# Layer 1 attention: key projections taken from among the scores into the weighing

## The reference, cut to what matters

```python
q = split(xn @ Wq)                                # 16 heads, 1024 x 64
k = concat([split(xn @ Wkv[:, :1024]), split(ctx @ Wm)])
v = concat([split(xn @ Wkv[:, 1024:]), split(ctx @ Wm)])
attn = softmax(q @ k.T * 64 ** -0.5)              # 1024 x 7428 for each head
x = x + tanh(g) * (heads(attn @ v) @ Wo + bo)
```

## Time and profile before

| | |
|---|---|
| median of 3 runs | 5230.36 us (5229.31 to 5230.93) |
| profiled execution, its own time | 5229.35 us |
| its span | 5227.6 us |
| PE busy in the span | 4813.3 us (92%) |
| DVE busy | 4069.5 us (78%) |
| ACT busy | 3357.1 us (64%) |
| POOL busy | 1961.0 us (38%) |
| L960, projections, in the stretch 440 to 2700 us | 238 matmuls |
| L1018, weighing | 3024 matmuls |

### The profile page before, as it was taken

The page is one execution under the profiler, slowest core; times in us unless marked ns, Lnnn a source line. Parts: engine busy times, 40 slices in busy tenths (PEclk is TensorE's granted clock), DMA queues, the critical chain, the costliest instruction groups (busy, mean ns, idle before and its releaser), DMA issues. The chain is left out here.

```text
span 5227.6 us, 76770 instructions
## 1 busy us (share of the span) xinstructions
PE 4813.3 (92%) x26366; PEld 1882.8 (36%) x26366; DVE 4069.5 (78%) x4870; ACT 3357.1 (64%) x6623; POOL 1961.0 (38%) x1522
## 2 busy tenths in 40 slices
PE   8938999999999999999994699999998699999997
PEld 5623454545445454544442222222222222222222
DVE  7646767677676767677776699999995599999996
ACT  3314565666666566656651388888885288888886
POOL 0015878787787878788782100000000100000000
PEclk9978999999999999999996799999998699999998
DMA  1024334242333334242210311111110211111110
GB/s 36 5 88 120 95 95 112 63 123 54 110 75 99 95 90 117 55 126 56 52 30 16 81 32 29 29 29 29 29 23 2 79 29 29 29 32 32 29 23 6
DMA packets 171390, 298.23 MB, mean 57 GB/s; under 512 B 39060, under 2 KB 108576, under 8 KB 167392
## 3 DMA queue, kind: packets, MB, share of 16 engines
q1 hardware_dynamic: 169420, 292.95, 22.0%
q10 hardware_dynamic: 1584, 0.37, 0.0%
HBM read 187.39 MB, written 101.25 MB: 55 GB/s over the span
## 5 line engine op out<-in xcount | busy, mean ns | idle before, releaser
L1856 ACT ACTIVATE a_prob<-ps 128x512 f32<-128x512 f32 (+1 forms) x3264 | 1699.4, 602 | 289.0 <-PE ps L1736 284.2
L1914 DVE TENSOR_REDUCE a_mx<-ps 128x1 f32<-128x1024 f32 x1536 | 1815.1, 1220 | 70.6 <-PE ps L1748 55.0
L1283 POOL TENSOR_TENSOR tot_p<-tot_p,prob 128x512 f32<-128x512 f32 (+1 forms) x922 | 1300.6, 1411 | 353.6 <-ACT prob L1141 267.6
L1748 PE MATMUL ps<-a_K,a_Q 59*128 59x512 bf16 (+1 forms) x3328 | 1094.7, 386 | 56.6 <-DMA a_Q<-q_stack_dram 44.7
L1141 ACT ACTIVATE prob<-ps 128x512 f32<-128x512 f32 (+1 forms) x1512 | 801.4, 609 | 511.7 <-PE ps L1007 510.7
L1736 PE MATMUL ps<-a_Q,a_K 59*128 59x512 bf16 (+1 forms) x3264 | 988.7, 383 | 55.3 <-ACT a_prob L1856 49.1
L1772 PE MATMUL ps<-a_prob,a_V 128*9 128x512 f32 x6528 | 872.1, 596 | 10.9 <-ACT a_acc L1840 10.9
L1006 PE MATMUL ps<-QA,KA 128*128 128x512 f32 (+1 forms) x1888 | 841.7, 446 | 0.0
L1018 PE MATMUL ps<-prob,V 128*64 128x512 f32 x3024 | 801.1, 599 | 0.7 <-ACT prob L1141 0.7
L1007 PE MATMUL ps<-QB,KB 128*128 128x512 f32 (+1 forms) x1888 | 746.6, 395 | 0.0
L1224 DVE TENSOR_TENSOR tot_d<-tot_d,prob 128x512 f32<-128x512 f32 x539 | 619.4, 1149 | 146.0 <-ACT prob L1141 129.5
(11 more groups left out here) (419 smaller groups left out, 4341.4 us busy)
## 6 DMA issues: line engine op xcount, KB each, us to landing
a_K<-k_stack_dram SPq DMA_DIRECT2D x128, 300.2 KB
k_hi_dram<-hi_s SPq DMA_DIRECT2D x112, 256.0 KB, 2.1
k_lo_dram<-lo_s SPq DMA_DIRECT2D x112, 256.0 KB, 2.4
KA<-k_hi_dram SPq DMA_DIRECT2D x64, 384.0 KB, 4.3
KA<-k_lo_dram SPq DMA_DIRECT2D x64, 384.0 KB, 5.6
KB<-k_hi_dram SPq DMA_DIRECT2D x64, 384.0 KB, 6.6
k_bf_dram<-bf_s SPq DMA_DIRECT2D x112, 128.0 KB, 1.8
KM<-k_bf_dram SPq DMA_DIRECT2D x32, 448.0 KB, 5.5
```

Source lines behind the costliest of these rows:

```text
L1283: nc.gpsimd.tensor_tensor(tot_p[0:r, u % 2, :], tot_p[0:r, u % 2, :], p, ALU.add).then_inc(totalled_p, 1)
L1748: last = nc.tensor.matmul(c.banks(slot(step) + half)[:, 0:k], Q[u % 3][MROW:MROW + ROWS, j * P:(j + 1) * P], K[(u // HALVES) % 2][MROW:MRO ...
L1856: nc.scalar.activation(prob[0:r, batch % 2, t % BATCH, :], c.banks(n % 3)[0:r, :], ACT.Exp, scale=SCALE).then_inc(exped, 1)
L1914: nc.vector.tensor_reduce(mx[:, u % 2, j, i % FULL:i % FULL + 1], c.banks(slot(step), 2), AX.X, ALU.max).then_inc(maxed, 1)
```

## The change

The key jobs leave `extras_of` and get a function of their own, `keys_of`, with the same rounds and the same jobs. In PE's list they go from behind the fourth and sixth score into `weigh`, behind its fourth and sixth tile (`KEYS_BEHIND = (3, 5)`). Their slot numbers are taken behind the second two maximum steps. On ACT, DVE and POOL the key's instruction goes to the end of the round, on SP behind the round's segment loads.

```diff
@@ -645,7 +645,7 @@
     LIFTED = 4
     BEFORE_WEIGHING = [n for n in range(STEPS) if n % 4 < 2 and n not in (0, 1, 4, 5)] + [2, 3]
     FIN_AT, NM_AT = 1, ROUNDS - 1
-    EXTRAS_BEHIND = (3, 5)
+    EXTRAS_BEHIND, KEYS_BEHIND = (3, 5), (3, 5)
     SEG = 12
     SEGS = -(-TILES // SEG)
     ACC = 3
@@ -693,12 +693,15 @@
             found.append(("fin", u - 1))
         if i == 0 and p >= 1 and r < 2:
             found += [("v", (p, g)) for g in ((GROUPS - 3, GROUPS - 2), (GROUPS - 1,))[r]]
-        if p + 1 < PAIRS:
-            if i < 2 and 2 <= r < 7:
-                found += [("k", (p + 1) * JOBS + k) for k in range(9 * i + 2 * (r - 2), min(9 * i + 2 * (r - 1), 9 + 8 * i))]
-            if i == 3 and r >= 2:
-                found += [("v", (p + 1, 2 * (r - 2) + n)) for n in range(2)]
+        if p + 1 < PAIRS and i == 3 and r >= 2:
+            found += [("v", (p + 1, 2 * (r - 2) + n)) for n in range(2)]
         return found
+
+    def keys_of(u, r):
+        p, i = divmod(u, 4)
+        if p + 1 < PAIRS and i < 2 and 2 <= r < 7:
+            return [(p + 1) * JOBS + k for k in range(9 * i + 2 * (r - 2), min(9 * i + 2 * (r - 1), 9 + 8 * i))]
+        return []
 
     def max_steps(u, r, part):
         first = STEPS * (u + 1) + LEAD + (4 * r - 2 if r else 0) + 2 * part
@@ -726,6 +729,8 @@
                 takes_slot(*extra)
             for step in max_steps(u, r, 1):
                 takes_slot("max", step)
+            for k in keys_of(u, r):
+                takes_slot("k", k)
     takes_slot("fin", UNITS - 1)
 
     def slot(n):
@@ -930,12 +935,11 @@
                     if u % 4 == 2 and u + 2 < UNITS:
                         load_wo(u // HALVES + 1)
                     for r in range(ROUNDS):
-                        for kind, what in extras_of(u, r):
-                            if kind == "k":
-                                store(what)
                         for v, t in scored_in(u, r):
                             if v % HALVES == 1 and v + 1 < UNITS and (t % SEG == SEG - 1 or t == TILES - 1):
                                 load_segment(v // HALVES + 1, t // SEG)
+                        for k in keys_of(u, r):
+                            store(k)
                     if u + 2 < UNITS:
                         load_q(u + 2)
                     if u % HALVES == 1 and (u + 3) // 2 < HEADS:
@@ -1006,19 +1010,23 @@
                     nc.tensor.matmul(out, KA[:, cols], QA[u % 2][:], start=True, stop=False)
                     nc.tensor.matmul(out, KB[:, cols], QB[u % 2][:], start=False, stop=True).then_inc(scored, 1)
 
-                def weigh(u, tiles):
+                def weigh(u, tiles, keys=()):
                     pe.wait_ge(exped, ring_no(u, tiles[-1]) + 1)
                     if tiles[0] == 0 and u >= 1:
                         pe.wait_ge(acc_out, u)
                     p, side = u // 4, (u // HALVES) % 2
                     if u % 4 == 0:
                         pe.wait_ge(v_out, freed[slot_no["v", (p, tiles[-1] // BATCH)]][1])
-                    for t in tiles:
+                    keys = dict(zip(KEYS_BEHIND, keys))
+                    for n, t in enumerate(tiles):
                         g = t % 2
                         last = nc.tensor.matmul(c.banks(ACC)[DH * g:DH * (g + 1), :],
                                                 V[:, t, DH * side:DH * (side + 1)], prob_of(u, t), start=(t < 2),
                                                 stop=(t + 2 >= TILES), skip_group_check=True)
-                    last.then_inc(weighed, 1)
+                        if n == len(tiles) - 1:
+                            last.then_inc(weighed, 1)
+                        if n in keys:
+                            project(keys[n])
 
                 def finish(u):
                     bank = take_slot(slot_no["fin", u])
@@ -1036,9 +1044,7 @@
                     last.then_inc(slotted, 1)
 
                 def extra(kind, what):
-                    if kind == "k":
-                        project(what)
-                    elif kind == "v":
+                    if kind == "v":
                         project_v(*what)
                     else:
                         finish(what)
@@ -1066,7 +1072,7 @@
                         for step in max_steps(u, r, 1):
                             max_score(*step)
                         if weighed_in(u, r):
-                            weigh(*weighed_in(u, r))
+                            weigh(*weighed_in(u, r), keys_of(u, r))
                 score(UNITS - 1, TILES - 1)
                 weigh(*weighed_in(UNITS, 0))
                 finish(UNITS - 1)
@@ -1142,9 +1148,7 @@
                                          ).then_inc(exped, 1)
 
                 def take_extra(kind, what):
-                    if kind == "k":
-                        round_hi(what)
-                    elif kind == "v":
+                    if kind == "v":
                         take_v(*what)
                     else:
                         take_fin(what)
@@ -1171,6 +1175,8 @@
                             take_nm(u + 1)
                         for step in max_steps(u, r, 1):
                             lift(*step)
+                        for k in keys_of(u, r):
+                            round_hi(k)
                         if r == 0 and u >= 1:
                             take_acc(u - 1)
                 exponential(UNITS - 1, TILES - 1)
@@ -1232,9 +1238,7 @@
 
                 nc.vector.memset(c.y[:], 0.0).then_inc(y_clear, 1)
                 def take_extra(kind, what):
-                    if kind == "k":
-                        cut_lo(what)
-                    elif kind == "fin":
+                    if kind == "fin":
                         invert(what)
 
                 for k in range(JOBS):
@@ -1255,6 +1259,8 @@
                             take_extra(*what)
                         for step in max_steps(u, r, 1):
                             maximum(*step)
+                        for k in keys_of(u, r):
+                            cut_lo(k)
                 invert(UNITS - 1)
 
             @block.gpsimd
@@ -1301,9 +1307,7 @@
                     nc.gpsimd.tensor_tensor(y, y, share, ALU.add).then_inc(added, 1)
 
                 def take_extra(kind, what):
-                    if kind == "k":
-                        cast(what)
-                    elif kind == "fin":
+                    if kind == "fin":
                         add_up(what)
 
                 for k in range(JOBS):
@@ -1318,6 +1322,8 @@
                                 take_extra(*extras.pop(0))
                         for what in extras:
                             take_extra(*what)
+                        for k in keys_of(u, r):
+                            cast(k)
                 total_up(UNITS - 1, TILES - 1)
                 add_up(UNITS - 1)
 
```

## The result

| | before | after |
|---|---|---|
| median of 4 runs each | 5230.64 us | 5331.45 us (5324.97 to 5332.47) |
| ratio to before | | 1.0191, 95% interval 1.0173 to 1.0208 |
| span of the profiled execution | 5227.6 us | 5330.7 us |
| PE busy | 4813.3 us (92%) | 4869.9 us (91%) |
| DVE busy | 4069.5 us (78%) | 4190.5 us (79%) |

The change costs 101 us. The forecast was 5320 (5268 to 5348), 90 us more than before.

The account below looks back on a forecast made before the run. PE was taken as the bound, its waits and added work counting one for one. 56 rounds with two projections at +1.45 us (81) and 7 with one at +1.29 (9) gave +90 us: 5320, range 5268 to 5348.

Parts of the forecast that it names:

- (a): In weighing, the first projection waits for DVE's read of the third maximum step: PE stands still for 1.11 us.
- W: The start of weighing in a round on PE; W+2.68 means 2.68 us after it.
- (b): The second projection waits for the read of the fourth maximum step; claimed to be met, without a wait.
- (c): The next round's first maximum step waits for the first projection's slot, free at W+5.35; claimed to be met.
- The changes of form: PE's switches between 64-column weighing and 128-column projections or maximum steps: 0.14 us claimed for each.
- (d): The next round's second maximum step waits for the second projection's slot: 0.25 us, where a wait of 0.36 stood before.
- The sum: Rounds with two projections 12.20 us against 10.75, +1.45; rounds with one 10.81 against 9.52, +1.29.
- At nothing: ACT's copy, POOL's casts and SP's stores, moved later in the round, were counted as costing no time.
- Rival 1: DVE reads the third maximum step early, so (a) vanishes while changes of form stay: +29 us, 5259; chance 0.08.
- rival 2: Changes of form on PE cost nothing, (a) as forecast: +74 us, 5304; chance 0.22.
- rival 3: Changes of form on PE cost 0.33 us each: +108 us, 5339; chance 0.15.
- Rival 4: DVE's read is done by W+1.57, form costs nothing, the present 0.36 wait goes: -17 us, 5213; chance 0.04.

Follow-up runs that it names:

- e1: The changed kernel with DVE's reads of the third and fourth maximum step ahead of its third total in rounds with keys: 5273.46 us, ratio 1.0085.
- e2: The changed kernel with both projections of a round next to each other behind the fourth tile: 5293.16 us, ratio 1.0125.
- e6: The kernel before with all extras (keys, value projections, finishes) behind the third and fifth score instead of fourth and sixth: 5209.59 us, ratio 0.9960.
- e5: The changed kernel with e1's order on DVE and both projections behind the fourth tile: 5237.03 us, ratio 1.0015.
- e7: The kernel before with only the key projections one score earlier, behind the third and fifth: 5207.31 us, ratio 0.9960.

## Why the prediction was right, point by point

- **(a), the wait for DVE's read.** Forecast: read ends at W+2.68, projection at W+2.83. Measured: W+2.70 and W+2.80 (median 2.79). The choice between the earlier trace rows, the largest in the sum, was right: without keys among the scores DVE's frame is that of the plain round. The reason given for it, that projections stretch the scoring, is only part; the last section shows the other, DVE's slower totals, which the forecast took in by taking the whole of the earlier trace rows. e1 takes the wait away and 55 us with it. By the waits of PE it stands in all 63 rounds.
- **(b) and (c), met.** No wait is marked at the second projection or at the next round's first maximum step.
- **The changes of form.** Forecast 0.14 each, measured 0.15 to 0.20 in the timeline and 0.17 in e2. The Trainium skill, page "TensorEngine Tiling (Array Packing)", section "Key Properties" (the prediction calls it its constraints), says that changing the tiling mode drains the TensorE; this case's trace agrees with it in kind, and puts a number beside it: 0.86 of work takes 1.01 to 1.06 (771.72 to 772.73, 772.73 to 773.79). The weight loads of the changed kernel show that they no longer run ahead:

```profile
770.66 0.30 PEld L964 LDWEIGHTS ps<-hT,weights 128*128 128x128 f32 x2 [1.71 <-issue]
771.72 0.20 PEld L1023 LDWEIGHTS ps<-h,V 128*64 128x64 f32 x4 [0.76 <-issue]
772.73 0.30 PEld L964 LDWEIGHTS ps<-hT,weights 128*128 128x128 f32 x2 [0.81 <-issue]
```

  The load at 772.73 starts with its matmul, where that of the earlier trace rows ran 0.23 ahead. Whether the 0.17 is an emptying of the array or just a load that nothing covers, no run here separates: a full load alone takes 0.19 in the scores.
- **(d), the second maximum step.** Forecast 0.25; measured 0.55 instead of 0.27 at the step itself, which is 0.28 (from the projection's start to the step it took 2.62, 772.73 to 775.35, where 2.52 was forecast, and the maximum steps came 0.07 later), and 0.34 for the half round by the medians of e2's comparison. The idle mark (0.16) shows less than half of it, since it counts from the modelled end of the step before, which lies past the usual start of the next. The wait of the kernel before shows the same: a mark of 0.24, 0.36 in the prediction's reading, 0.43 when e6 took it away.
- **The sum.** Forecast 12.20 for a double round; measured 12.40 in the round shown, 12.36 as the median of the 49 with two full jobs. The 0.16 is made of 0.07 up to the maximum steps (6.90 against 6.83, the dearer changes of form less a slightly shorter (a)) and of 0.09 from there to W (5.46 against 5.37). Kind by kind, before and after: 49 rounds from 10.74 to 12.36, 79 us; the seven with the short job from 9.94 to 11.60, 12 us; the seven single rounds 1.27 more each, 9 us. That is 100 of the 101 us. The seven short ones were counted like the other doubles, +1.45, and cost +1.65: they had no wait before that the change could end. No step failed; two terms were taken somewhat small, the change of form by the nearest row of a cheaper kind, (d) by a chain taken 0.10 too short and by 0.06 behind the step that it left out. Apart from 0.03 in (a) the errors lie on one side, so the 11 us are not what is left of larger errors.
- **At nothing.** ACT's, POOL's and SP's moved work made no wait that PE shows. DVE's busy time rose by 121 us for the same instructions, which no step had; its total of 4190 us still leaves room, and the rounds without keys are as long as before (median 8.70 in both). PE's share of busy time in 1000 to 1500 us is 97%, where some 96% was forecast.
- **Rivals.** Rival 1 is e1: forecast +29, measured +46. Its sum had the same two small terms: 11.23 for a double round, median 11.46, which is 11 of the 17 us, and the same shortcut for the rounds with the short job, 2 more. The price of nothing for the change of form (rival 2, 5304) is ruled out by e2, that of 0.33 (rival 3, 5339) by the rows. Rival 4, the gain, would have needed the read by W+1.57; e1 makes that so and is still slower than before, because the changes of form and (d) remain; e5, without (d) too, is still 8 us slower. The gain itself was real, 20 us (17 in the prediction), and e6 and e7 collect it in the old place.

## What to carry to other kernels

A filler for TensorE is best placed by two questions: whose result frees its buffer, and does its shape match its neighbours'. Here moving it past two takers of a ring of two slots turned a wait worth 0.43 us into one worth 0.90 (e1) behind an engine that had three other things to do first, and its 128 columns among 64-column work cost 0.17 at each border. An idle mark in the profile can show half of what a wait costs; the length of the round with and without it tells. When a filler's consumer is late, try one step earlier in the same surroundings before giving it a new home.

## What the runs showed of the hardware that was not expected

DVE's totals became slower without being touched. Line L1224 of before, and L1230 of the changed kernel, 440 to 2700 us, duration as least, median, most:

```profile
L1224 DVE TENSOR_TENSOR tot_d<-tot_d,prob x519: 681/1115/1598, 444.1 to 2699.4; 128x512 f32<-128x512 f32 x173
```

```profile
L1230 DVE TENSOR_TENSOR tot_d<-tot_d,prob x492: 691/1400/1599, 447.1 to 2694.9; 128x512 f32<-128x512 f32 x164
```

The same 128 x 512 add takes 0.68 us at best and 1.60 at most; the median rose from 1.115 to 1.400. Over the whole kernel these adds took 771.5 us before and 882.9 after, 111 of the 121 us by which DVE's busy time rose. All of it lies in the rounds with keys, where the mean of one rose from 0.90 to 1.49; in the others it is 1.23 in both. The Trainium skill, page "SBUF — State Buffer", section "Who interferes with whom", says that a VectorE instruction with two SBUF inputs contends with a GpSimd instruction that reads SBUF. DVE's add reads both its inputs from SBUF, and POOL's adds read there at the same time. The trace agrees, down to single instructions. One pair of the changed kernel:

```profile
767.90 1.53 POOL L1289 TENSOR_TENSOR tot_p<-tot_p,h 128x512 f32<-128x512 f32 x1
768.41 1.58 DVE L1230 TENSOR_TENSOR tot_d<-tot_d,prob 128x512 f32<-128x512 f32 x1
```

POOL's ends at 769.43 and DVE's at 769.99, 0.56 later. Of the 615 adds of DVE in this window every one starts while a POOL instruction runs, and 573 end 0.54 to 0.56 behind its end; the other 42 begin when it has 0.07 to 0.11 to go, and take 0.69. So an add lasts as long as POOL's instruction still has to run, and 0.55 more. In the kernel before, 576 of 649 do the same. This is a pattern in the traces; no run here took POOL's adds away. What the change altered in the rounds with keys is how much POOL still has to run when DVE begins: while the scores had projections among them it was little, and with the scores in one piece it is mostly about 1.0.

This is part of why DVE's read ends at W+2.70 now, while in the double round of the earlier trace rows it ended at 765.35, W+1.19. The three totals ahead of it take 4.27 now; there they took 1.10, 0.69 and 1.14, 2.93 in all. Their lengths alone come to 1.34 of the 1.51 by which the read is later:

```profile
759.71 1.10 DVE L1224 TENSOR_TENSOR tot_d<-tot_d,prob 128x512 f32<-128x512 f32 x1
...
761.81 0.69 DVE L1224 TENSOR_TENSOR tot_d<-tot_d,h 128x512 f32<-128x512 f32 x1
...
763.61 1.14 DVE L1224 TENSOR_TENSOR tot_d<-tot_d,prob 128x512 f32<-128x512 f32 x1
764.67 0.68 DVE L1197 CUSTOM_DVE_ANT_0 over<-ps,over 128x512 bf16<-128x512 f32 x1
```
